# Layer 3 attention: the order of key blocks, four places for the carried maxima, and the next input's load moved behind four carries

## The reference

```python
logits = jnp.einsum('bqhd,bkhd->bhqk', Q, K) * scale
logits = jnp.where(causal, logits, -jnp.inf)
attn = jax.nn.softmax(logits, axis=-1)
...
gated = attn * gate[:, None, None, :]
out = jnp.einsum('bhqk,bkhd->bqhd', gated, V).reshape(B, S, E)
return out @ Wo + bo
```

## Time and profile before

| What | Value |
|---|---|
| median of 3 runs | 3875.83 us (3875.41 to 3878.35) |
| profiled execution | 3882.36 us, span 3880.6 us |
| layer 3 attention, four times | about 159, 160, 158 and 157 us |
| TensorE busy over the whole span | 3373.7 us (87%) |
| SyncE carries (L1274) | 512 DMAs, 0.5 KB each, 2.0 us from issue to landing |

### The profile page before, as it was taken

One profiled execution on the slowest core, in us unless ns is written; L12 is line 12 of the kernel. 1 busy time (PEld: TensorE's weight loads), 2 busy tenths in 40 slices (PEclk: granted clock), 3 DMA queues, 4 the chain that ended last, 5 costly groups with the idle time before them and its releaser, 6 DMA issues. The chain is left out here.

```text
span 3880.6 us, 51281 instructions
## 1 busy us (share of the span) xinstructions
PE 3373.7 (87%) x18610; PEld 2435.7 (63%) x18610; DVE 2080.9 (54%) x3463; ACT 1466.3 (38%) x2638; POOL 830.2 (21%) x908
## 2 busy tenths in 40 slices
PE   6996898988988989888989698998988789888898
PEld 4555655975568755875569445555454477777776
DVE  4446744686455954667446574655647434343333
ACT  2321144412443134421444355463644433333333
POOL 1112322742246411643127101001010000000000
PEclk9997899988998999998999789898998899899999
DMA  5111100110011100210001200000001120000000
GB/s 179 41 45 60 38 1 30 45 45 22 1 51 47 44 1 1 74 34 33 1 30 48 63 2 13 12 7 18 2 12 12 61 94 6 17 11 12 11 12 11
DMA packets 139735, 121.01 MB, mean 31 GB/s; under 512 B 79696, under 2 KB 121936, under 8 KB 136016
## 3 DMA queue, kind: packets, MB, share of 16 engines
q1 hardware_dynamic: 139472, 117.45, 9.9%
HBM read 100.23 MB, written 28.31 MB: 33 GB/s over the span
## 5 line engine op out<-in xcount | busy, mean ns | idle before, releaser
L1375 ACT ACTIVATE l3b_prob<-sums 128x512 f32<-128x512 f32 (+3 forms) x768 | 337.8, 497 | 280.7 <-PE sums L1308 224.3
L1623 PE MATMUL sums<-l4a_uhi,l_h 128*128 128x512 f32 x1024 | 405.2, 396 | 0.0
L1623 PE MATMUL sums<-l4a_ulo,l_h 128*128 128x512 f32 x1024 | 404.0, 395 | 0.0
L842 POOL TENSOR_TENSOR l2c_rlo<-l2c_routed,l2c_rhi 128x512 fp32r<-128x512 f32 x256 | 348.1, 1373 | 216.0 <-ACT l2c_rhi L868 178.6
L769 DVE TENSOR_REDUCE l2b_mx<-sums 128x1 f32<-128x1024 f32 (+7 forms) x256 | 192.1, 758 | 316.5 <-PE sums L650 315.8
L703 ACT ACTIVATE l2b_prob<-sums 128x512 f32<-128x512 f32 (+3 forms) x384 | 186.4, 491 | 394.8 <-PE sums L666 390.0
L1668 DVE TENSOR_TENSOR l4a_ulo<-l4a_made,l4a_uhi 128x512 fp32r<-128x512 f32 x192 | 132.3, 689 | 375.2 <-ACT l4a_uhi L1636 374.3
L222 POOL COPY sb_x<-sb_nx 128x2048 f32<-128x2048 f32 x12 | 23.0, 1914 | 1383.6 <-issue 604.6
L952 PE MATMUL sums<-l2c_ohi,l2c_rhi 128*128 128x256 f32 x1024 | 295.2, 288 | 12.8 <-POOL l2c_rlo L842 11.9
L1303 PE MATMUL sums<-l_qst,l_kst 64*128 64x512 f32 (+3 forms) x768 | 290.6, 440 | 17.2 <-DMA l_qst<-l3b_peak 9.9
L674 PE MATMUL sums<-l2b_prob,l_vx 128*128 128x512 f32 (+3 forms) x768 | 301.0, 506 | 3.3 <-ACT l2b_den L725 1.9
(11 more groups left out here) (247 smaller groups left out, 8170.7 us busy)
## 6 DMA issues: line engine op xcount, KB each, us to landing
l_ve<-ve SPq DMA_DIRECT2D x34, 512.0 KB, 4.1
l_oe<-oe SPq DMA_DIRECT2D x16, 1024.0 KB, 5.9
sb_nx<-sums SPq DMA_DIRECT2D x15, 1024.0 KB, 5.6
l2c_word<-weights_copy SPq DMA_DIRECT2D x32, 352.0 KB, 3.6
weights_copy<-h SPq DMA_DIRECT2D x2, 4096.0 KB, 26.2
l_qst<-l3b_peak SPq DMA_DIRECT2D x512, 0.5 KB, 2.0
l_h<-weights_copy SPq DMA_DIRECT2D x2, 4096.0 KB, 23.9
sb_nx<-tokens SPq DMA_DIRECT2D x5, 1024.0 KB, 5.6
```

Of the source, the lines that this page charges most:

```text
L842: pool.tensor_tensor(rlo[:, i % RT, :], routed[:, i % RT, :], rhi[:, i % RT, :].bitcast(F32), ALU.subtract).then_inc(s.routed_lo, 1)
L1375: act.activation(prob[:, i % RB, j, a, 0:hi - lo], bank(m.ps, part % SCORE, 0, hi - lo), ACT.Exp, scale=SCALE1).then_inc(s.exp_ready, 1)
L1623: run(lambda out, a, x, first, last: pe.matmul(out, a, x, start=first, stop=last))
```

## The change

Four things are edited in `attention`, all for layer 3 only:

1. The key blocks of a chunk are taken in turn from both ends: 0, 7, 1, 6, 2, 5, 3, 4 for n = 1 and 0, 3, 1, 2 for n = 0. The last block of a chunk (`keys[n][-1]`) is then 4 or 2, and the copy out is tied to that one.
2. `peak` gets four places (RP = 4), and VectorE waits for the landing of sub u-4.
3. `shifted` becomes two semaphores, one for even and one for odd subs, and SyncE no longer waits for the landing of the sub just issued but, before the DMAs of sub u, for that of sub u-2.
4. The load of the next input stands behind the DMAs of sub 3.

```diff
-        peak = sb("peak", [P, 2, 2, TPH], F32R)
+        peak = sb("peak", [P, RP, 2, TPH], F32R)
...
-        steps = [(c, k) for c, (g, n) in enumerate(chunks) for k in range(TPH * (n + 1))]
+        keys = [[0, 3, 1, 2], [0, 7, 1, 6, 2, 5, 3, 4]]
+        steps = [(c, k) for c, (g, n) in enumerate(chunks) for k in keys[n]]
...
-        carried = lambda u: 16 * CARRIES * (u + 1)
+        carried = lambda u: 16 * CARRIES * (u // 2 + 1)
+        shifted = (s.even_shifted, s.odd_shifted)
...
-        finish_in = {steps.index((c, k)): c for c, k in steps if k == TPH * (chunks[c][1] + 1) - 1}
+        finish_in = {steps.index((c, keys[n][-1])): c for c, (g, n) in enumerate(chunks)}
...
-                fetch_load(sp, m, sf, src[(b + 1) % SEQS])
                 for u, (p, n) in enumerate(subs):
+                    if u >= 2:
+                        sp.wait_ge(shifted[u % 2], carried(u - 2))
                     if n:
                         sp.wait_ge(s.combined, combined_to(u))
...
-                                         peak[:, u % 2, a, j:j + 1].bitcast(F32)).then_inc(s.shifted, 16)
-                    sp.wait_ge(s.shifted, carried(u))
+                                         peak[:, u % RP, a, j:j + 1].bitcast(F32)).then_inc(shifted[u % 2], 16)
+                    if u == 3:
+                        fetch_load(sp, m, sf, src[(b + 1) % SEQS])
...
-                    pe.wait_ge(s.shifted, carried(2 * c + j))
+                    pe.wait_ge(shifted[j], carried(2 * c + j))
...
-                    if n == 0 and u >= 2:
-                        dve.wait_ge(s.shifted, carried(u - 2))
+                    if n == 0 and u >= RP:
+                        dve.wait_ge(shifted[u % 2], carried(u - RP))
...
-                        dve.wait_ge(s.shifted, carried(u - 2))
+                        if u >= RP:
+                            dve.wait_ge(shifted[u % 2], carried(u - RP))
```

More of the change, by code:

```diff
@@ L971 @@
          "g_ready g_gelu gate_in gate_ready vx_ready")
-ATTN3 = "max_mm max_read combined shifted score_mm exp_ready pv_mm o_read"
+ATTN3 = "max_mm max_read combined even_shifted odd_shifted score_mm exp_ready pv_mm o_read"
 OUT3 = "bias_added turned rden o_ready turned_back oT_ready out_mm y_ready y_out"
@@ L1216, in attention @@
         TPH = HALF // P
-        LAG, AHEAD, RB, WARM, CARRIES = 2, 4, 5, 2, 8
-        peak = sb("peak", [P, 2, 2, TPH], F32R)
+        LAG, AHEAD, RB, WARM, CARRIES, RP = 2, 4, 5, 2, 8, 4
+        peak = sb("peak", [P, RP, 2, TPH], F32R)
         low, high = sb("low", [P, 2, 2, TPH]), sb("high", [P, 2, 2, TPH])
@@ L1361, in out @@
                     g, n = chunks[c]
-                    act.wait_ge(s.pv_mm, steps.index((c, TPH * (n + 1) - 1)) + 1)
+                    act.wait_ge(s.pv_mm, steps.index((c, keys[n][-1])) + 1)
                     act.copy(oraw[:, g, n * HALF:(n + 1) * HALF], bank(m.ps, PV)).then_inc(s.o_read, 1)
@@ L1382, in _ @@
                     p, n = subs[u]
-                    out = (peak if n == 0 else low if lo == 0 else high)[:, u % 2, :, t % TPH]
-                    if n == 0 and u >= 2:
-                        dve.wait_ge(s.shifted, carried(u - 2))
+                    out = (peak[:, u % RP] if n == 0 else (low if lo == 0 else high)[:, u % 2])[:, :, t % TPH]
+                    if n == 0 and u >= RP:
+                        dve.wait_ge(shifted[u % 2], carried(u - RP))
                     dve.wait_ge(s.max_mm, i + 1)
@@ L1389, in _ @@
                         dve.wait_ge(s.max_read, i + 1)
-                        dve.wait_ge(s.shifted, carried(u - 2))
-                        dve.tensor_tensor(peak[:, u % 2, :, :], low[:, u % 2, :, :], high[:, u % 2, :, :],
+                        if u >= RP:
+                            dve.wait_ge(shifted[u % 2], carried(u - RP))
+                        dve.tensor_tensor(peak[:, u % RP, :, :], low[:, u % 2, :, :], high[:, u % 2, :, :],
                                           ALU.max).then_inc(s.combined, 1)
```

## The result

The changed kernel takes 3912.82 us (median of 4 runs, 3904.88 to 3919.61), the kernel before on the same chip 3875.62 us: a ratio of 1.0097, 95% interval 1.0073 to 1.0122. It is 37 us slower; 28 were worked out and 3902 forecast.

What follows compares the result with a forecast made beforehand. TensorE is busy for 87% of the span, so only time between products or the clock can be won. Terms -3.3 + 11.6 - 5.4 + 4.2 = +7.1 us a sequence, +28 in all, gave 3904, taken as 3902; range 3858 to 3922.

Steps and rivals of the forecast that it cites:

- A: Stage start: sub 1's carry DMAs follow sub 0's at once, odd sub's first score product starts earlier; -3.3 us a sequence.
- The bound for a clock that falls less: Stage start, chunks 0 and 1: if the clock never falls there, -12 us a sequence instead of -3.3.
- B: Carry into the next chunk loses cover: waits of 2.7 to 3.5 us, +9.6 at chunks 2-5, +2.0 at chunk 7; +11.6.
- D: Clock falls behind four new waits, 1.2 us each, less 0.6 for falls already there in chunk 5; +4.2 us a sequence.
- C: Evener maxima in chunks 2 to 4 (-1.2 us each) and no VectorE wait for a place; -5.4 us a sequence.
- the place wait before sub 13: VectorE's 3.19 us wait for a place of the maxima, claimed to go; 1.8 us of it taken as on the path.
- R5: Rival: VectorE's waits for a place never were binding, C loses 1.8; 3911 us, within the forecast's 52%.
- no 3.5 us step without such a wait: Sign expected in the changed profile: steps show no 3.5 us one unless a carry wait stands there.
- R1: Rival: carry is covered and evener maxima win; 3845 us, or 3820 with the clock kept in chunks 0 and 1; 18%.
- R2: Rival: the carry waits come but the clock holds; +2.9 us a sequence, 3887 us; 12%.

Runs made afterwards that it cites:

- e2: The kernel before with only the new order of key blocks, nothing else changed: 3922.4 us, ratio 1.0109.
- e11: The changed kernel with two places for the carried maxima instead of four: 3920.4 us, ratio 1.0112.
- e5: The changed kernel with nine overwritten 512-column products before the odd sub's first score product in chunks 2, 3, 4, 5 and 7: 3887.1 us.
- e3: The changed kernel with maxima asked for eight tiles ahead of the scores instead of four: 3859.9 us, ratio 0.9954.
- e7: The changed kernel with the natural key-block order and maxima asked for eight tiles ahead instead of four: 3890.5 us, ratio 1.0035.
- e1: The changed kernel with the key blocks back in natural order, all other edits kept: 3864.5 us, ratio 0.9971.
- e4: The changed kernel with four carry DMAs a sub instead of eight, half the maxima left out (measurement only): 3823.9 us, ratio 0.9863.

## Why the prediction was right

**A, start: -3.3 worked out, -4.1 measured.** The odd score of chunk 0 starts 15.9 us after the stage, not 18.7, after 3.15 us idle, and the clock falls as before. But the number is right by luck, since the step behind it does not hold: in e2 the odd score still starts 18.3 to 18.8 us after the stage, and the start takes 45.5 us all the same. That the place wait of VectorE was part of it is wrong (e11), and that the order does nothing inside chunks 0 and 1 is wrong too (e2 gains 5.2 us there by itself). The bound for a clock that falls less was nearer to the point: of the changed kernel's four starts the one with 17.1 us at the low clock takes 44.0 us, the one with 36.4 takes 49.8. Which edit gives the 4.1, and what makes the low clock long or short, can't be told from these runs.

**B and D, chunks 2 to 5.** The mechanism was right in its place and its releaser, and a little over-sized: the waits were to be 2.7 to 3.5 us and are 2.36 to 2.65 in the first stage, and 1.70 at chunk 5. Ahead of chunk 4 the last step took 2.93 us (2302.52 to 2305.45) and not 2.6, so that there was more cover. D was under-sized: 4.2 worked out, 7.1 in the profiles and 6.5 by the medians of e5. One fall was counted per wait with 1.2 us each. The clock was low for 3.4 us behind five of the waits, about the one fall counted, and for 6.8 or 10.2 us behind eight; behind two of the sixteen waits, of 1.70 us (chunk 5, first stage) and of 2.39 us (chunk 3, third stage), it stayed at 1.00. The 0.6 us taken off for falls that two stages already had stands on no row shown; in the profile of before they are there, in the first and the third stage. e5 leaves +3.0 for B and C in these chunks, where 9.6 - 5.4 = 4.2 was worked out.

**C, -5.4: over-sized.** Where the carries are covered (e3), chunks 3 to 5 show -0.4, -1.0 and -1.3 against before, and chunk 2 +0.5, where C had -1.2 for each of chunks 2 to 4. Against e7, with the same lead, it is -4.6 for the four. The 1.8 us for the place wait before sub 13 was wrong. The late step at the end of chunk 4 that I took for its effect (3.20 us for block 5, where chunk 3 has 2.53) is still 3.20 in e1, which has four places; three tiles stand in that step, and two in chunk 3's. Rival R5 was right on this point. That its 3911 is the nearest of all is luck, as the errors below cancel. Chunk 4 also has a cost that I did not see. Its step of block 3 takes 4.11 us in the changed kernel (2325.26 to 2329.37) and 4.10 in e5:

```profile
2325.26 1.82 ACT L1379 ACTIVATE l3b_prob<-sums 128x512 f32<-128x512 f32 x3 [0.48 <-PE sums L1307]
2327.84 0.60 ACT L1379 ACTIVATE l3b_prob<-sums 128x512 f32<-128x512 f32 x1 [0.76 <-PE sums L1307]
2329.37 2.06 ACT L1379 ACTIVATE l3b_prob<-sums 128x512 f32<-128x512 f32 x4 [0.93 <-PE sums L1312]
```

Three tiles stand in it, the last of sub 11 and the first two of sub 12; TensorE waits 0.57 us for VectorE's reduction of sub 11 in the middle of it. This 1.4 us over the same step of chunk 3 (2.72) is one reason why the order's 3.5 us steps were not all won, and my "no 3.5 us step without such a wait" was wrong there. A part of it came back: the longer step is cover, and chunk 5's wait is the shortest.

**Chunk 7: +2.0 worked out, +3.2 measured**, for a wait of 4.00 us and the clock behind it. **Chunk 6** lost 0.5 us, which was counted at nothing: its first step takes 3.2 us and not 2.9.

The sum is +9.7 a sequence, not +7.1, and the sign, the place and the order of size come from B: D is too small by 2.9, chunk 7 by 1.2 and chunk 6 by 0.5; against that, A gave 0.8 more than worked out, and B and C together cost 1.2 less. So the sum missed by 2.6 us a sequence where its terms, taken singly, missed by 6.6: a part of the nearness is errors that cancel. R1 failed because the cover was two steps; e3 shows it to be right as soon as the cover is there. (Its 3820 does not follow from its own terms: -12 + 1 - 5.4 a sequence gives 3810.) R2 is excluded by the windows at 0.51. e5 puts its case at 3887, just its number, but by other parts: -2.4 at the start, +3.0 in chunks 2 to 5 and +3.2 in chunks 6 and 7, where R2 had -3.3, +4.2 and +2.0.

## What to carry to other kernels

Before work is made more even, ask what the uneven order was covering: here the last maxima of a chunk came three steps early, and their carry needed just that. Count a chain of small DMAs by its issue time on the queue, and move its producer forward, or make fewer DMAs of it, before adding places or groups in flight. Each of the four waits of about 2.2 us in front of TensorE cost another 1.8 us in the mean by the clock behind it (7.1 us for four), so fill such a wait or remove it.

## What the runs showed of the hardware

- A DMA of 128 elements from one SBUF place to another takes SyncE 0.60 to 0.62 us to issue (four 2.40, eight 4.97 us), with 5.25 and 5.79 us for eight at times; the score it releases starts 1.5 to 1.6 us after the last issue.
- A TensorE idle time of 2.65 us, in a 3.15 us stretch with 0.50 us of products, was followed by a stretch at 0.51. With nine products of 512 columns in 2.33 us of the wait, the chunk stayed at 1.00, and the kernel was 26 us faster.
- The fall is not bound to a wait of that length. In e4, 1.21 us idle before chunk 2's odd score was followed by 6.8 us at 0.5; in the third stage of the changed kernel, 2.39 us idle before chunk 3's was followed by none.
